# A fused attention and expert kernel: x1's sum on GpSimd, router and expert biases by a matmul, one gathering operation, and other steps for the splitting of q

## What is computed

```python
x = x + xattn0(layernorm(x), ctx, ctx)   # 8 heads of 16 rows; attention between the 256 columns
x = x + ffn0(layernorm(x), router_w, router_b, expert_w, expert_b)  # 16 experts pick 128 tokens each
x = x + xattn1(layernorm(x), ctx, mask)  # softmax over 128 context rows
x = x + ffn1(layernorm(x), w_r, b_r, w1, b1, w2, b2)  # half of the tokens, gelu
# xattn0, for each head: q, k, v are [16, 256]; softmax over n of (q.T @ k) / 4
#   ret[c, m] = sum_n softmax[m, n] * v[c, n]
# ffn0: logits = x @ router_w + router_b; out = tokens @ expert_w + expert_b, weighted and added back
```

## Time and profile before

| | |
|---|---|
| three runs | 419.33, 420.0, 426.34 us (median 420.0) |
| profiled execution, time | 422.43 us |
| its span, first to last instruction | 420.2 us |
| mean granted TensorE clock | 0.841 of full |
| busy, share of the span | PE 67%, PEld 43%, DVE 76%, ACT 40%, POOL 23% |

### The profile page before, as it was taken

How to read it: one execution, slowest core, us unless ns; L and a number is a source line. 1 busy time by engine, 2 the same in 40 slices (tenths; PEclk the granted TensorE clock), 3 DMA queues, 4 the chain that set the end, 5 groups by cost and what they waited for, 6 DMA issues and landing times.

```text
span 420.2 us, 7370 instructions
## 1 busy us (share of the span) xinstructions
PE 279.6 (67%) x1872; PEld 182.5 (43%) x1872; DVE 317.7 (76%) x989; ACT 167.6 (40%) x397; POOL 94.8 (23%) x222
## 2 busy tenths in 40 slices
PE   1134777777886877877778621001559999999996
PEld 0011333353442544444334310000438988888884
DVE  5847458899989889799986748888377888787631
ACT  4110543464654536464556500000111566445631
POOL 1101323352415224111111110000133322333200
PEclk9999975789698886899989965555555999999999
DMA  2789388959294581740000380000000000000001
GB/s 88 202 189 153 98 221 187 166 150 165 71 197 79 145 126 54 146 80 1 2 1 2 100 301 0 1 0 2 1 0 0 2 25 25 25 0 25 26 27 51
DMA packets 24379, 32.90 MB, mean 78 GB/s; under 512 B 4066, under 2 KB 22434, under 8 KB 22818
## 3 DMA queue, kind: packets, MB, share of 16 engines
q1 hardware_dynamic: 23842, 32.48, 33.5%
q10 hardware_dynamic: 512, 0.13, 0.2%
HBM read 24.02 MB, written 8.39 MB: 77 GB/s over the span
## 4 chain that ended last, share of the span: by engine, by line
DVE 35%; PE 33%; issue 12%; DMA 8%; ACT 4%; POOL 3%; SPq 2%; DVEq 1%; ACTq 1%; POOLq 0%
DVE row_max L531 7%; PE t_bank L1355 5%; PE pv_bank L1273 5%; PE pv_bank L1121 4%; DMA q_stack<-q_parts_dram 4%; DVE denom_inv L549 3%; PE score_bank L1094 3%; PE scoret_bank L1107 3%; PE t_bank L1150 2%; PE score_bank L1336 2%; DMA q_parts_dram<-q_parts 2%; ACT probs L895 2%; DMA q_stack<-neg_max 2%; PE score_bank L1303 2%; DVE junk L705 1%
## 5 line engine op out<-in xcount | busy, mean ns | idle before, releaser
L895 ACT ACTIVATE probs<-scoret_bank 128x512 f32<-128x512 f32 x128 | 73.1, 596 | 52.5 <-PE scoret_bank L1107 42.3
L531 DVE TENSOR_REDUCE row_max<-score_bank 128x2 f32<-128x512 f32 x112 | 74.4, 679 | 24.3 <-PE score_bank L1094 23.1
L1107 PE MATMUL scoret_bank<-q_stack,k_stack 98*128 98x256 bf16 (+1 forms) x256 | 54.6, 301 | 28.1 <-ACT probs L895 18.7
L1094 PE MATMUL score_bank<-k_stack,q_stack 96*128 96x256 bf16 (+1 forms) x240 | 53.6, 314 | 19.1 <-DMA q_stack<-q_parts_dram 11.0
L355 POOL TENSOR_SCALAR var_eps<-mv 128x1 f32<-128x1 f32 x48 | 9.2, 192 | 189.5 <-DVE mv L567 106.9
L1107 PEld LDWEIGHTS scoret_bank<-q_stack,k_stack 98*128 98x128 bf16 (+1 forms) x256 | 24.2, 104 | 46.6 <-ACT probs L895 20.5
L1121 PE MATMUL pv_bank<-probs,values_ones 128*32 128x256 f32 x512 | 42.0, 455 | 1.0 <-ACT probs L895 1.0
L1094 PEld LDWEIGHTS score_bank<-k_stack,q_stack 96*128 96x128 bf16 (+1 forms) x240 | 21.7, 105 | 47.8 <-issue 15.3
L1273 PE MATMUL pv_bank<-q_stack,k_stack 128*128 (+1 forms) x256 | 36.0, 285 | 0.4 <-ACT q_stack L1070 0.4
L1045 ACT COPY xnt<-score_bank 128x256 f32<-128x256 f32 x16 | 6.0, 373 | 74.6 <-PE score_bank L1294 74.6
L1273 PEld LDWEIGHTS pv_bank<-q_stack,k_stack 128*128 128x128 f32 x256 | 33.9, 202 | 1.3 <-issue 0.9
(11 more groups left out here) (182 smaller groups left out, 534.5 us busy)
## 6 DMA issues: line engine op xcount, KB each, us to landing
q_stack<-q_parts_dram SPq DMA_DIRECT2D x48, 128.0 KB, 6.9
k_parts_dram<-k_parts SPq DMA_DIRECT2D x24, 128.0 KB
q_parts_dram<-q_parts SPq DMA_DIRECT2D x24, 128.0 KB
k_stack<-k_parts_dram SPq DMA_DIRECT2D x8, 384.0 KB, 4.6
ctx_stage<-in_ctx_dram SPq DMA_DIRECT2D x8, 256.0 KB, 3.2
x_stage<-in_x_dram SPq DMA_DIRECT2D x8, 256.0 KB, 3.9
k_stack<-k_parts_dram SPq DMA_DIRECT2D x8, 256.0 KB, 5.3
xs<-in_x_dram SPq DMA_DIRECT2D x8, 256.0 KB, 7.3
```

The lines of the kernel that those rows point to most:

```text
L531: dve.tensor_reduce(row_max[:, i, :, h], score_bank[bank_of][:, :].rearrange("p (m n) -> p m n", m=2), AX.X, ALU.max).then_inc(s["max_done ...
L895: act.activation(probs[:, j % PROBS, :], scoret_bank[j % 2][:, :], ACT.Exp).then_inc(s["exp_done"], 1)
L1094: ins = pe.matmul(to[:, m * D:(m + 1) * D], q_stack[0:QROWS, slot, h, b_in, m * P:(m + 1) * P], k_stack[0:QROWS, slot, h, b_in, :], start= ...
L1107: ins = pe.matmul(scoret_bank[j % 2][:, k * D:(k + 1) * D], k_stack[0:SROWS, slot, h, b_in, k * P:(k + 1) * P], q_stack[0:SROWS, slot, h, ...
```

## The change

- **x1's sum** (`add_x1`) is made by GpSimd. It stands in GpSimd's list ahead of `root_rows`, behind four waits; VectorE keeps the statistics (`stats_x1`), at steps 6 and 14 instead of 5 and 13. `scale_rows` stays at 7 and 15.
- **Gathering** becomes one operation of 512 elements for each batch, by the column `high`, with both halves of `low_part`, which ScalarE fills from the other half of the bank (`take_even`). The result, `gathered`, holds denominator and numerator side by side, and the product by the inverse is written over the numerator.
- **Biases**: `expert_b` and `router_b` are loaded into three rows instead of 128. Once, in unit 0, GpSimd cuts them into three bf16 parts, one in each row (`split_bias`, ahead of the first `add_x1`). `yw` adds them by a third matmul of three rows of ones with them. ScalarE takes the 272 columns out by one copy (`take_yw`, steps 7 and 13) to `y_ext`, in which y and the logits lie side by side.
- **Splitting**: VectorE's `stats_q(u + 4)` goes from step 15 to 13, `scale_q(u + 3)` from step 1 to 0; ScalarE's `high_q` from 2 to 3, `mid_q` from 4 to 6, `take_vt` from 6 to 5 (unit 1: 4 to 5, 6 to 8, and 6 to 5); GpSimd's `low_q` goes from ahead of the odd batch's root to behind it, ahead of `keep_rows`.
- Not shown in the diff: work tiles of the last stage (`x_new3`, `z`, `attn` and others) lie in the two last slots of `k_stack`, which are free by then, and the softmax over experts writes its last result to `soft`.

```diff
-        y = sb("y", [P, NB, D])
+        y_ext = sb("y_ext", [P, NB, D + NE])
+        y = y_ext[:, :, 0:D]
...
-                for dst, row in ((eb_rows[:, 0:D], expert_b), (eb_rows[:, D:D + NE], router_b),
+                for dst, row in ((bias_f[:, 0:D], expert_b), (bias_f[:, D:D + NE], router_b),
...
-                    sp.dma_start(dst, row.rearrange("(a n) -> a n", a=1).to_broadcast([P, row.shape[0]])).then_inc(s["w_small"], 16)
+                    sp.dma_start(dst, row.rearrange("(a n) -> a n", a=1).to_broadcast([dst.shape[0], row.shape[0]])).then_inc(s["w_small"], 16)
...
+            def add_x1(b, u, i, first):
+                wait_apart(pool, s["div_step"], 4 * b + 4)
+                wait_apart(pool, s["x_loaded"], 16 * (u + 1))
+                if not first:
+                    wait_apart(pool, s["xn_ready"], b - 1)
+                    wait_apart(pool, s["kept"], b - 1)
+                pool.tensor_tensor(x_new[:, i, :], gathered[:, i, 1, :], xs[:, b, :], ALU.add).then_inc(s["x1_done"], 1)
+
             def keep_rows(rows, b, i):
                 pool.tensor_copy(xs[:, b, :], rows[:, i, :]).then_inc(s["kept"], 1)
+
+            def split_bias():
+                n = [0]
+
+                def step(ins):
+                    n[0] += 1
+                    ins.then_inc(s["bias_step"], 1)
+                    pool.wait_ge(s["bias_step"], n[0])
+
+                pool.wait_ge(s["w_small"], 16 * 9)
+                step(pool.tensor_copy(bias_terms[:, 0, :], bias_f[:, :]))
+                step(pool.tensor_tensor(bias_left[:, 0, :], bias_f[:, :], bias_terms[:, 0, :], ALU.subtract))
+                step(pool.tensor_copy(bias_terms[:, 1, :], bias_left[:, 0, :]))
+                step(pool.tensor_tensor(bias_left[:, 1, :], bias_left[:, 0, :], bias_terms[:, 1, :], ALU.subtract))
+                step(pool.tensor_copy(bias_terms[:, 2, :], bias_left[:, 1, :]))
+                for part in range(3):
+                    wait_apart(pool, s["ident_done"], 1)
+                    ins = pool.tensor_scalar(bias_kept[:, part, :], bias_terms[:, part, :], ident[0:3, part:part + 1], None, ALU.mult)
+                step(ins)
+                step(pool.tensor_tensor(bias_sum[:, :], bias_kept[:, 0, :], bias_kept[:, 1, :], ALU.add))
+                pool.tensor_tensor(bias_parts[:, :], bias_sum[:, :], bias_kept[:, 2, :], ALU.add).then_inc(s["bias_done"], 1)
...
                 fill_values(2 * u + 1, u, 1, first)
-                if parts and not first:
-                    low_q(u + 3)
                 if not first:
+                    add_x1(2 * u - 1, u - 1, 1, second)
                     root_rows(2 * u - 1, 1)
+                    if parts:
+                        low_q(u + 3)
                     keep_rows(x_new, 2 * u - 1, 1)
...
                     low_q(u + 3)
+                if first:
+                    split_bias()
+                add_x1(2 * u, u, 0, first)
                 root_rows(2 * u, 0)
...
             unit(NU - 1, False, False, False, False, True)
+            add_x1(NB - 1, NU - 1, 1, False)
             root_rows(NB - 1, 1)
...
             def gather_parts(b, i):
-                odd_heads = pv_bank[i][:, D:2 * D]
                 dve.wait_ge(s["even_taken"], b + 1)
-                dve.scalar_tensor_tensor(denom[:, i, :], odd_heads, low[:, 0:1], sum_high[:, i, :],
+                if not (isinstance(b, int) and b < 2):
+                    dve.wait_ge(s["x1_done"], b - 1)
+                dve.scalar_tensor_tensor(gathered[:, i].rearrange("p k n -> p (k n)"), pv_bank[i][:, :], high[:, 0:1],
+                                         low_part[:, i].rearrange("p k n -> p (k n)"),
                                          ALU.mult, ALU.add).then_inc(s["div_step"], 1)
-                dve.scalar_tensor_tensor(numer[:, i, :], odd_heads, high[:, 0:1], num_low[:, i, :],
-                                         ALU.mult, ALU.add).then_inc(s["div_step"], 1)
...
             def invert(b, i):
-                dve.wait_ge(s["div_step"], 5 * b + 1)
-                dve.reciprocal(denom_inv[:, i, :], denom[:, i, :]).then_inc(s["div_step"], 1)
+                dve.wait_ge(s["div_step"], 4 * b + 1)
+                dve.reciprocal(denom_inv[:, i, :], gathered[:, i, 0, :]).then_inc(s["div_step"], 1)
...
             def bring_over(b, i):
-                wait_apart(dve, s["div_step"], 5 * b + 3)
+                wait_apart(dve, s["div_step"], 4 * b + 2)
                 dve.stream_shuffle(out=denom_own[:, i, :], in_=denom_inv[:, i, :],
                                    mask=[(n + C) % Q for n in range(Q)]).then_inc(s["div_step"], 1)
-                dve.wait_ge(s["div_step"], 5 * b + 4)
-                dve.tensor_tensor(numer[:, i, :], numer[:, i, :], denom_own[:, i, :], ALU.mult).then_inc(s["div_step"], 1)
-
-            def add_x1(b, u, i, first):
-                dve.wait_ge(s["div_step"], 5 * b + 5)
-                dve.wait_ge(s["x_loaded"], 16 * (u + 1))
-                if not first:
-                    dve.wait_ge(s["kept"], b - 1)
-                dve.tensor_tensor(x_new[:, i, :], numer[:, i, :], xs[:, b, :], ALU.add).then_inc(s["x1_done"], 1)
+                dve.wait_ge(s["div_step"], 4 * b + 3)
+                dve.tensor_tensor(gathered[:, i, 1, :], gathered[:, i, 1, :], denom_own[:, i, :],
+                                  ALU.mult).then_inc(s["div_step"], 1)
+
+            def stats_x1(b, i):
                 dve.wait_ge(s["x1_done"], b + 1)
...
                                   ALU.subtract, ALU.mult).then_inc(s["xn_ready"], 1)
-
-            def take_yw(b):
-                dve.wait_ge(s["yw_ready"], b + 1)
-                if is_n(b, 0):
-                    dve.wait_ge(s["w_small"], 16 * 9)
-                dve.tensor_tensor(y[:, b, :], t1_bank[:, 0:D], eb_rows[:, 0:D], ALU.add)
-                dve.tensor_tensor(logits[:, b, :], t1_bank[:, D:D + NE], eb_rows[:, D:D + NE], ALU.add).then_inc(s["yw_done"], 1)
...
                         stats_q(u + 3)
-                    if j == (3 if second else 1) and not first and parts:
+                    if j == (3 if second else 0) and not first and parts:
                         scale_q(u + 3)
...
                         bring_over(a, 1)
-                    if j == 5 and not first:
-                        add_x1(a, u - 1, 1, second)
+                    if j == 6 and not first:
+                        stats_x1(a, 1)
                     if j == 7 and not first:
                         scale_rows(a, 1, second)
-                    if j == 8 and not first:
-                        take_yw(2 * u - 2)
                     if j == 10 and scored and not first:
...
                         bring_over(b, 0)
-                    if j == 13:
-                        add_x1(b, u, 0, first)
-                    if j == 14 and not first:
-                        take_yw(a)
+                    if j == 14:
+                        stats_x1(b, 0)
                     if j == 15:
                         scale_rows(b, 0, first)
-                    if j == 15 and more_parts and not first:
+                    if j == 13 and more_parts and not first:
                         stats_q(u + 4)
...
-            add_x1(NB - 1, NU - 1, 1, False)
-            take_yw(NB - 2)
+            stats_x1(NB - 1, 1)
...
-            take_yw(NB - 1)
...
+            def take_yw(b):
+                act.wait_ge(s["yw_ready"], b + 1)
+                act.copy(y_ext[:, b, :], t1_bank[:, 0:D + NE]).then_inc(s["yw_done"], 1)
+
             def high_k(u):
...
                 if not first:
-                    act.wait_ge(s["div_step"], 5 * (b - 1))
-                act.mul(sum_high[:, i, :], pv_bank[i][:, 0:D], high[:, 0:1])
-                act.mul(num_low[:, i, :], pv_bank[i][:, 0:D], low[:, 0:1]).then_inc(s["even_taken"], 1)
+                    act.wait_ge(s["div_step"], 4 * (b - 2) + 1)
+                act.mul(low_part[:, i, 0, :], pv_bank[i][:, D:2 * D], low[:, 0:1])
+                act.mul(low_part[:, i, 1, :], pv_bank[i][:, 0:D], low[:, 0:1]).then_inc(s["even_taken"], 1)
...
                         take_xnt(2 * u - 2, 0, second)
-                    if j == (4 if second else 2) and parts:
+                    if j == (5 if second else 3) and parts:
                         high_q(u + 3)
-                    if j == (6 if second else 4) and parts:
+                    if j == (8 if second else 6) and parts:
                         mid_q(u + 3)
-                    if j == 6 and parts:
+                    if j == 5 and parts:
                         take_vt(u + 3)
+                    if j == 7:
+                        take_yw(2 * u - 2)
                     if j == 9:
                         take_even(2 * u, 0, False)
+                    if j == 13:
+                        take_yw(2 * u - 1)
                     if j == 10 and not last:
...
+            take_yw(NB - 2)
...
+            take_yw(NB - 1)
...
                     if not first:
```

(9 more changed lines are left out.)

43 lines of the change are left out of this document (24 added, 19 removed).

## The result

| | before | changed |
|---|---|---|
| median (runs) | 423.16 us (4) | 432.75 us (4) |
| lowest to highest | 419.33 to 426.34 | 429.66 to 434.08 |
| profiled execution, span | 422.43, 420.2 | 431.88, 430.1 |
| mean granted TensorE clock | 0.841 | 0.832 |
| busy share PE, DVE, ACT, POOL | 67, 76, 40, 23% | 67, 71, 40, 26% |

The changed kernel takes 1.0301 times as long, 95% interval 1.0201 to 1.0402: slower by 3%, where no measurable change was forecast. The time of one kernel varies by several us from run to run, so single profiles are read for waits and their places, and ratios decide. A run more than 1.5% above the fastest of its kernel is left out of every ratio: here the two of the kernel before at 426.3 us, which is why the ratio isn't that of the two medians, and further down also the profiled runs of kernels 11 and 15, so that their rows count less.

What follows compares the result with a forecast made beforehand. VectorE, 76% busy, was taken to bound the attention stage, an engine-to-engine chain its last unit. Terms -0.7 -0.4 -0.7 +0.2 +0.4 +0.95 = -0.25 us gave 422.2 profiled, 419.8 median; 8-in-10 range 413 to 426.5.

Steps and rivals of the forecast that it cites:

- A unit that also splits q and k: Units 2, 3 and 4 of the attention stage: 0 for unit 2, -0.2 us each for 3 and 4.
- units 0 and 1: Start of the attention stage: -0.3 us as VectorE's stand is covered, -0.4 for a sum no longer beside low_q.
- unit 5: Attention unit without splitting: first half gains 0.45 us, second nothing, two gathers 0.26; sum -0.7 us.
- unit 7: Last attention unit: x1 over GpSimd costs 0.7 less 0.15, y's copy saves 0.45, bias matmul adds 0.25; +0.4 us.
- ScalarE is better off by 0.45: Units that split, ScalarE: the exponential of step 3 no longer waits for qn, a gain of 0.45 us.
- So the first half's xn loses 0.8: Units that split, VectorE: moved low_q runs beside the first half's xn, +0.8 us; the second half's gains 0.8.
- late stage loads: Rival, slower: late x_stage holds VectorE's queue, 4 us, and a lower TensorE clock adds 2.6; 426.5 us; chance 0.15.
- VectorE stands 0.7 us, for each batch: Between mv and xn: one maximum fills GpSimd's 1.4 us road for the root; of 1.0 us saved, 0.3 is left.
- Hidden, with nothing to spare: x1's sum on GpSimd: there 1.5 us after the product's start, VectorE asking at 1.54, behind two maxima.
- The biases: Unit 0, GpSimd's splitting of the biases: 6.3 us, done near 75, VectorE's 2 us stand covered by TensorE's late score.
- signs of being wrong: Units 5 and 6 shorter by over 1 us, maxima waiting for TensorE instead, or the half-clock share before 250 us changing much.
- the saving stays: Rival, faster: VectorE keeps its 1.0 us for 12 batches of units 1 to 6; 409.5 us, with half 415.5; chance 0.15.

Runs made afterwards that it cites:

- kernels 11 and 15: 11: the kernel before with the single gathering alone, 422.93 us, ratio 1.0075. 15: kernel 5 with x1's statistics at 6 and 14, 421.93 us, 0.9953.
- kernels 3 and 12: 12: kernel 3 with ScalarE's rounding of q ahead of sending the negative maxima in step 3, 413.71 us, ratio 0.9857.
- kernel 3: The changed kernel with x1's sum and statistics back on VectorE at steps 5 and 13, splitting steps still moved: 413.99 us, ratio 0.983.
- the table of eight: All combinations of x1's sum (VectorE or GpSimd), its statistics (early or late) and splitting steps (old or moved), gathering and biases as changed: ratios 0.9805 to 1.0301.
- kernel 6: The changed kernel with GpSimd's low_q alone put back ahead of x1: 434.85 us, ratio 1.0328.
- kernel 5: The changed kernel with all splitting steps put back and x1's sum and statistics back on VectorE at 5 and 13: 412.99 us, ratio 0.9805.

## Why the prediction was wrong

**The step that failed** is "A unit that also splits q and k": "0 for unit 2 and -0.2 each for 3 and 4: -0.4". Measured over these units' six halves (batch 3 to 9) it is +4.1, and over the stretch from batch 2 to 8 +5.9. All terms, from the reciprocals of the two profiled runs:

| term of the sum | predicted | measured |
|---|---|---|
| units 0 and 1 (to batch 3) | -0.7 | +2.1 |
| units 2, 3 and 4 (3 to 9) | -0.4 | +4.1 |
| unit 5 (9 to 11) | -0.7 | -0.7 |
| unit 6 (11 to 13) | +0.2 | +0.3 |
| unit 7 (13 to 15) | +0.4 | +2.4 |
| the end (15 to lg_max) | +0.95 | +0.95 |
| behind lg_max | 0 | +0.8 |

Inside unit 2 the chain on VectorE and GpSimd came out to the tenth: mv at 3.15 (predicted 3.3), qn from 7.19 to 8.74 (7.3 to 8.7), the reciprocal over at 13.2 (139.73 + 1.73 - 128.28; 13.2), xn beside low_q 1.15 (1.18). What was wrong was to close the account where VectorE's chain ends: the loss comes behind it, in the half from the reciprocal of batch 5 to that of batch 6, which took 13.99 us for 12.55 before, with TensorE at the lower clock level and VectorE waiting for it (2.01 us).

- "ScalarE is better off by 0.45 (the exponential of step 3 no longer waits for qn)." The exponential of step 3 did come 0.4 us earlier (8.97 for 9.34). But in its new step the rounding of q stands behind two DMA issues that wait for VectorE's neg_max: it came 3.1 us later, and the exponential behind it 0.9 us later (12.47 for 11.53). Only SP's DMAs had been costed, not ScalarE's own. That this costs little by itself is seen at kernels 3 and 12; it takes away slack, which the late x1 then wants (1.0301 against 1.0015; that it is this slack, of the moved steps' several, is argued and not shown: ScalarE's steps back alone gave 1.0222).
- "So the first half's xn loses 0.8 and the second half's, which then meets only a short copy, gains 0.8." xn was costed as VectorE's time. But TensorE's transposition waits for it (1.72 at 150.01), so 0.62 for the root and 0.74 for the longer scaling come one behind the other on TensorE's path. The lock alone isn't the cause: in kernel 3 xn takes 1.16 or 1.17 us in batches 3, 5 and 7, as here, and that kernel is faster than the one before. Taking the odd batch's statistics forward brought 9 us.
- The clock was taken as given. A rival had priced it, 2.6 us for a unit at 0.74 instead of 0.87 by the earlier trace rows, but tied it to late stage loads. Here it was 0.74 and 0.75 in two stretches of 26 and 27 us with no late load, and before it fell TensorE had idled for xn and an exponential (1.11 us busy of 4). In the table of eight the clock falls about as the time rises. Which is cause and which effect of a lower clock and a longer stretch the runs don't part, nor how much of the 2.6% is waits and how much clock. It stays open. So does which of the six moved steps meets the late statistics: put back alone, ScalarE's three gave 1.0222, GpSimd's one 1.0328, and VectorE's two a spread of 419 to 430 us.

**The second mis-sized term is x1's move**: "VectorE stands 0.7 us, for each batch" against 0.45 saved, so +0.25 a batch, +4 us in all. The stand itself was right: 0.59 to 0.68 in each of batches 1 to 11. The move cost 2.3% (0.9805 to 1.0038 with the old steps), 9.8 us. xn is late for TensorE as well; where the statistics are early, VectorE waits for GpSimd instead (14.0 us, less 16 times 0.42 saved, is 7.3, and the pair of 0.983 and 1.0015 is 7.8 us apart).

**The account in three terms**, each by ratio times 421 us: gathering and biases -8.2 (VectorE's 0.41 and 0.13 for sixteen batches would be -8.6, about the same, but the parts don't fit one by one, as the gathering alone gained nothing; TensorE's 8.2 of waiting for the logits may be the same time seen from its side); x1's sum and its late statistics +9.8 (predicted +4); the moved splitting steps on top of these +11.1 (predicted about 0). Sum +12.7, which is the 3.0% measured.

**What held, term by term.**
- x1 on GpSimd: 0.72 us (0.69 taken). "Hidden, with nothing to spare" is right for batches 1 to 11, whose statistics didn't wait for it. Those of batch 0 did, 1.02, and of batches 12 to 15, 1.22 or 1.23 each.
- The single gathering is 0.66 from start to start (0.65 taken; 123.62 to 124.28), but as an edit by itself it gained nothing.
- Unit 5: -0.7 from batch 9 to 11, as predicted. The table's -1.9 from 8 to 12 all lies from 8 to 10, more than half of it (-1.1, batch 8 to 9) in the share of unit 4. xn at 199.80 stood 0.66 for rstd.
- Unit 6 came as predicted; unit 7 did not, +2.4 for +0.4. Road and root, 1.22 and 1.23, stand bare in batches 12, 13 and 14, where one was reckoned with; and two of TensorE's operations ran at the lower level, 1.81 and 2.09 us (at 240.72 and 242.46) for 1.07 and 1.18 before, worth 1.65. That part changes from run to run: from batch 12 to 15 kernel 6, with the same edits there, took 22.1 us where the changed kernel took 25.3.
- The end: +1.0 for +0.95.
- The biases: 7.7 us for 6.3, with 1.02 of wait at the statistics (st at 77.26), as their cover was 1.5 of work and TensorE's lateness. The first stretch's +1.6 is rather the stacks' data, for which the maximum at 71.21 waited 3.33 us (1.61 before, at 69.61); another 0.7 comes from batch 2 to 3, in unit 1, which splits too.
- Stage loads: x_stage was issued at 123.20 and was there for the statistics at 129.22, which stood for nothing. That rival is out.
- The lock on the port: the Trainium skill ("SBUF — State Buffer", on the two separate sides) said what the trace shows, 1.15 us against 0.41. By it alone the loss of each unit would be 0.8; kernel 3 has the long xn and no loss (0.983), so as a price it is real and as the cause it is not.

Of the prediction's signs of being wrong, two came: VectorE's waits for TensorE before a maximum grew from 11.8 to 14.6 us, and the clock fell. The rival "the saving stays" is about kernel 5, 412.99 us: it was in reach, if x1 had stayed where it was.
